# State-space rows 1-4, 6, 7: two of eight pairs get their scan inputs from GpSimd and keep their decays in PSUM

## The reference, cut to what matters

```
x, z   = split(hidden @ W_in)                    # after the norm
u      = gelu(conv4(x)), z = gelu(conv4(z))      # 4 taps along l
dt, B, C = split(u @ W_xproj)
delta  = softplus(dt @ W_dt + b_dt)
h[l]   = exp(delta[l] * A[n]) * h[l-1] + delta[l] * B[n, l] * u[l]   # per d and n
y[l]   = sum over n of C[n, l] * h[l] + D * u[l]
out    = concat(y, z) @ W_out
```

## Time and profile before

| what | value |
|---|---|
| median of 3 executions | 879.94 us (879.92 to 880.79) |
| the profiled execution, its time | 881.1 us |
| its span, first to last instruction | 879.1 us |
| mean granted TensorE clock | 0.994 |
| busy: PE, DVE, ACT, POOL | 842.9, 700.3, 556.5, 629.0 us |
| first scan starts, last scan ends | 334.7, 566.6 us |

### The profile page before, as it was taken

One profiled execution on the slowest core, in us unless ns is written; L12 is line 12 of the kernel. 1 busy time (PEld: TensorE's weight loads), 2 busy tenths in 40 slices (PEclk: granted clock), 3 DMA queues, 4 the chain that ended last, 5 costly groups with the idle time before them and its releaser, 6 DMA issues. The chain is left out here.

```text
span 879.1 us, 12640 instructions
## 1 busy us (share of the span) xinstructions
PE 842.9 (96%) x3851; PEld 638.1 (73%) x3851; DVE 700.3 (80%) x1279; ACT 556.5 (63%) x1048; POOL 629.0 (72%) x471
## 2 busy tenths in 40 slices
PE   8999999999999999889898996999999999999997
PEld 7678778877877785566565554687887888788885
DVE  6969768777976578999999999877977877786664
ACT  6665655565557669878888784365565556555554
POOL 7959676766766767768886996865767667676765
PEclk9999999999999999999999999999999999999999
DMA  8733574363434343444344444345457435436440
GB/s 213 227 114 107 154 192 120 115 154 123 135 105 124 104 129 119 158 142 157 120 171 144 134 148 145 122 132 162 112 164 198 128 116 144 159 108 183 141 121 24
DMA packets 125139, 122.40 MB, mean 139 GB/s; under 512 B 59272, under 2 KB 82960, under 8 KB 125072
## 3 DMA queue, kind: packets, MB, share of 16 engines
q1 hardware_dynamic: 102368, 116.35, 43.9%
q10 hardware_dynamic: 22704, 5.25, 2.8%
HBM read 112.40 MB, written 9.18 MB: 138 GB/s over the span
## 5 line engine op out<-in xcount | busy, mean ns | idle before, releaser
L806 POOL TENSOR_TENSOR act_lo<-act,act_hi 128x512 fp32r<-128x512 f32 x288 | 372.4, 1298 | 187.4 <-ACT act_hi L917 185.4
L910 ACT ACTIVATE bank<-bank 128x512 f32<-128x512 f32 x252 | 146.6, 582 | 234.1 <-PE bank L1245 222.8
L1141 DVE TENSOR_TENSOR sg<-bank,c_ring 128x512 f32<-128x512 f32 x252 | 172.6, 685 | 97.1 <-ACT bank L910 95.1
L1241 PE MATMUL bank<-x_parts,w_hi 128*128 128x512 f32 x572 | 231.4, 405 | 3.1 <-DVE sg L1141 2.0
L1119 DVE SCALAR_TENSOR_TENSOR act<-sg,bank 128x512 f32<-128x512 f32 x288 | 197.9, 687 | 40.9 <-PE bank L1245 20.5
L1242 PE MATMUL bank<-x_parts,w_lo 128*128 128x512 f32 x572 | 226.2, 395 | 0.0
L1245 PE MATMUL bank<-x_parts,w_hi 128*128 128x512 f32 x572 | 226.2, 395 | 0.0
L917 ACT ACTIVATE act_hi<-act 128x512 fp32r<-128x512 f32 x286 | 178.1, 623 | 0.4 <-PE bank L1217 0.4
L1241 PEld LDWEIGHTS bank<-x_parts,w_hi 128*128 128x128 f32 x572 | 107.5, 188 | 35.2 <-issue 4.8
L1245 PEld LDWEIGHTS bank<-x_parts,w_hi 128*128 128x128 f32 x572 | 107.5, 188 | 25.9
L1242 PEld LDWEIGHTS bank<-x_parts,w_lo 128*128 128x128 f32 x572 | 107.6, 188 | 25.7 <-issue 1.7
(11 more groups left out here) (181 smaller groups left out, 959.1 us busy)
## 6 DMA issues: line engine op xcount, KB each, us to landing
c_ring<-c_dram SPq DMA_DIRECT2D x252, 256.0 KB, 3.7
c_ring<-c_dram SPq DMA_DIRECT2D x64, 512.0 KB, 3.7
y_dram<-out_t SPq DMA_DIRECT2D x56, 64.0 KB, 2.8
y_tok<-y_dram SPq DMA_DIRECT2D x14, 256.0 KB, 3.7
xt_dram<-xn ACTq DMA_DIRECT2D x40, 64.0 KB, 3.4
xt<-xt_dram ACTq DMA_DIRECT2D x10, 256.0 KB, 2.9
out<-x_sb SPq DMA_DIRECT2D x7, 256.0 KB, 2.4
x_sb<-in_L_attn_hidden_states SPq DMA_DIRECT2D x3, 512.0 KB, 6.5
```

The source lines that it names most:

```text
L806: self.nc.gpsimd.tensor_tensor(m["act_lo"][:, g % LAG], m["act"][:, g % ACTS], m["act_hi"][:, g % LAG].bitcast(FP32), ALU.subtract).then_i ...
L910: nc.scalar.activation(self.h_bank[:, g % 2], self.h_bank[:, g % 2], ACT.Silu).then_inc(self.sg_ready, 1)
L1141: nc.vector.tensor_tensor(m["sg"][:, g % 2], silu, weight, ALU.mult).then_inc(self.w_done, 1)
L1241: nc.tensor.matmul(dst, m["w_hi"][:, k, n, :], x_hi, start=True, stop=False)
```

## The change

In pairs 3 and 5 of rows 1, 2, 3, 4, 6 and 7, twelve pairs in all, the roles of the two operands change places. B comes to the partitions by a DMA from DRAM into one of two new SBUF slots (`b_slots`), as C does; GpSimd multiplies the slot by du in place; ScalarE writes the decays into the PSUM bank that B's spread used; and TensorE puts a single column of zeros into that bank (a matmul of one column) in place of the two spread matmuls. VectorE does nothing for the input of such a pair. To have B in DRAM, the store of C's rows becomes a store of B's and C's rows, issued at pair 3 of the row before. GpSimd multiplies slot 0 (for pair 3) at pair 7 of the row before, slot 1 (for pair 5) at pair 1 of the same row; its du of the next row moves from pair 3 to pair 4. On ScalarE the second copy of y moves behind the decays of its step. On TensorE one tap of z's convolution moves from step 5 to step 4.

```diff
+MOVED = ((),) + ((3, 5),) * 4 + ((),) + ((3, 5),) * 2
+SLOTS = 2
...
+    def store_rows(self, sp, i):
+        sp.wait_ge(self.rows_copied, 2 * (i + 1))
+        sp.dma_start(self.c_dram[i], self.bc_rows[0:2 * NS, :]).then_inc(self.c_stored, 16)
+
+    def load_slot(self, sp, i, n):
+        if n >= len(MOVED[i]):
+            return
+        earlier = [j for j in range(i) if len(MOVED[j]) > n]
+        if earlier:
+            sp.wait_ge(self.scan_done, earlier[-1] * PAIRS + MOVED[earlier[-1]][n] + 1)
+        else:
+            sp.wait_ge(self.f1.down_done, BLOCKS)
+        pair = MOVED[i][n]
+        sp.dma_start(self.m["b_slots"][:, n].rearrange("p s l -> p (s l)"),
+                     self.c_dram[i, 2 * pair:2 * pair + 2].rearrange("s l -> (s l)").partition_broadcast(P)
+                     ).then_inc(self.slot_loaded[n], 16)
...
+                if i + 1 < BATCH:
+                    if n == 3:
+                        self.store_rows(sp, i + 1)
+                    if n == 5:
+                        sp.wait_ge(self.c_stored, 16 * (i + 2))
+                        self.load_slot(sp, i + 1, 0)
+                    if n == 7:
+                        self.load_slot(sp, i + 1, 1)
...
+    def pool_input(self, pool, i, n):
+        if n >= len(MOVED[i]):
+            return
+        uses = self.slot_uses(i, n) + 1
+        pool.wait_ge(self.slot_loaded[n], 16 * uses)
+        slot = self.m["b_slots"][:, n]
+        self.nc.gpsimd.tensor_tensor(slot, self.m["du"][:, i % 2].unsqueeze(1).broadcast_to([P, 2, SEQ]), slot, ALU.mult
+                                     ).then_inc(self.slot_ready[n], 1)
...
-                    if n == (3 if i else 4):
+                    if n == 4:
                         self.pool_du(pool, i + 1)
+                    if n == 7:
+                        pool.wait_ge(self.du_ready, i + 2)
+                        self.pool_input(pool, i + 1, 0)
+                if n == 1:
+                    self.pool_input(pool, i, 1)
...
+        if self.moved(g):
+            ae.wait_ge(self.b_ready, g + 1)
+            for s in range(2):
+                nc.scalar.activation(self.b_of(g)[:, s, s:SEQ], m["delta"][:, i % 2, s:SEQ], ACT.Exp,
+                                     scale=m["a_neg"][:, 2 * n + s:2 * n + s + 1]).then_inc(self.decay_ready, 1)
+            return
...
+                if RING <= g + 1 < ALL_PAIRS and self.moved(g + 1):
+                    self.act_decays(ae, g + 1)
+                if RING <= g + 2 < ALL_PAIRS and not self.moved(g + 2):
+                    self.act_decays(ae, g + 2)
                 if n == 4 and i - 1 in TURNED:
                     self.act_back_y(ae, i - 1)
-                if RING <= g + 2 < ALL_PAIRS:
-                    self.act_decays(ae, g + 2)
...
+                if self.moved(g):
+                    slot = self.slot_of(g)
+                    dve.wait_ge(self.slot_ready[slot], self.slot_uses(i, slot) + 1)
+                    decays, added = self.b_of(g)[:], self.m["b_slots"][:, slot]
+                else:
+                    dve.wait_ge(self.in_done, self.inputs_before(g + 1))
+                    decays, added = self.decay[:, g % RING], self.b_of(g)[:]
...
+        if self.moved(g):
+            pe.wait_ge(self.zeroed, 1)
+            self.nc.tensor.matmul(self.b_of(g)[:, 1, 0:1], m["ident"][:, :], self.decay[:, 0, 0, 0:1], start=True,
+                                  stop=True).then_inc(self.b_ready, 1)
+            return
...
+                    if n == 4 and i:
+                        self.pe_conv(pe, i, 1, [1], self.z_bank(i))
                     if n == 5 and i:
-                        self.pe_conv(pe, i, 1, [1, 2], self.z_bank(i))
+                        self.pe_conv(pe, i, 1, [2], self.z_bank(i))
```

More of the change, by code:

```diff
@@ L108, in program @@
         act_hi = sb("act_hi", [P, LAG, SEQ], F32R)
+        with nc.sbuf_tensor("b_slots", [P, SLOTS, 2, SEQ], FP32) as b_slots:
+            pass
         act_lo = sb("act_lo", [P, LAG, SEQ], F32R)
@@ L117, in program @@
         xt_dram = nc.dram_tensor("xt_dram", (2, BATCH, D, SEQ), FP32, kind="Internal").ap()
-        c2_dram = nc.dram_tensor("c2_dram", (BATCH, NS, SEQ), FP32, kind="Internal").ap()
+        c2_dram = nc.dram_tensor("c2_dram", (BATCH, 2 * NS, SEQ), FP32, kind="Internal").ap()
         th = sb("th", [P, 2, P])
@@ L1382, in __init__ @@
         self.c_loaded = [sem(f"c_loaded{n}") for n in range(RING)]
+        self.slot_loaded = [sem(f"slot_loaded{n}") for n in range(SLOTS)]
+        self.slot_ready = [sem(f"slot_ready{n}") for n in range(SLOTS)]
         self.delta_ready, self.du_ready = sem("delta_ready"), sem("du_ready")
@@ L1399, in b_of, with moved, slot_of, slot_uses @@
         return self.b_bank[g % 2] if g else self.m["bank"][2]
+    def moved(self, g):
+        return g % PAIRS in MOVED[g // PAIRS]
+    def slot_of(self, g):
+        return MOVED[g // PAIRS].index(g % PAIRS)
+    def slot_uses(self, i, n):
+        return sum(len(pairs) > n for pairs in MOVED[:i])
+    def inputs_before(self, g):
+        return sum(not self.moved(j) for j in range(g))
+    def store_rows(self, sp, i):
[13 more added lines that the diff above has]
+                     ).then_inc(self.slot_loaded[n], 16)
     def load_c(self, sp):
         m = self.m
+        self.store_rows(sp, 0)
+        sp.wait_ge(self.c_stored, 16)
         for i in range(BATCH):
-            sp.wait_ge(self.rows_copied, 2 * (i + 1))
-            sp.dma_start(self.c_dram[i], self.bc_rows[NS:2 * NS, :]).then_inc(self.c_stored, 16)
-            sp.wait_ge(self.c_stored, 16 * (i + 1))
             for n in range(PAIRS):
@@ L1415, in load_c @@
                 sp.dma_start(slot.rearrange("p s l -> p (s l)"),
-                             self.c_dram[i, 2 * n:2 * n + 2].rearrange("s l -> (s l)").partition_broadcast(P)
+                             self.c_dram[i, NS + 2 * n:NS + 2 * n + 2].rearrange("s l -> (s l)").partition_broadcast(P)
                              ).then_inc(self.c_loaded[n % RING], 16)
+                if i + 1 < BATCH:
[6 more added lines that the diff above has]
+                        self.load_slot(sp, i + 1, 1)
     def pool_low_rows(self, pool, r):
@@ L1713, in dve_pairs @@
                 dve.wait_ge(self.decay_ready, 2 * g + 2)
-                dve.wait_ge(self.in_done, g + 1)
+                if self.moved(g):
[5 more added lines that the diff above has]
+                    decays, added = self.decay[:, g % RING], self.b_of(g)[:]
                 need(dve, self.sum_done, g - RING + 1)
@@ L1717, in dve_pairs @@
                     dve.wait_ge(self.f1.down_done, BLOCKS if g else BLOCKS - 2)
-                nc.vector.tensor_tensor_scan(flat(self.state(g)), flat(self.decay[:, g % RING]),
-                                             flat(self.b_of(g)[:]), 0.0, ALU.mult, ALU.add
+                nc.vector.tensor_tensor_scan(flat(self.state(g)), flat(decays), flat(added), 0.0, ALU.mult, ALU.add
                                              ).then_inc(self.scan_done, 1)
```

## The result

The changed kernel took a median of 882.52 us (880.89 to 883.78, 12 executions), the kernel before 879.97 us (878.69 to 882.57, 12 executions): a ratio of 1.0025, 95% interval 1.0015 to 1.0035. It is slower by 0.25%. The forecast was 871.2, so 11.3 us are to be explained.

The account below looks back on a forecast made before the run. VectorE was taken to pace rows 1 to 6, and row 7 until TensorE's last wait. Gains of 10.2 us, less 2.6 for GpSimd, plus 1.15 in row 7 gave 8.75, so 871.2 us by the median, range 868.5 to 874.

Parts of the forecast that it names:

- ACT: ScalarE's queue, rows 1 to 4: same number of exponentials, moved decays ready about in time; 0.5 us charged.
- signs of being wrong: Among them: VectorE waiting for ScalarE or TensorE over 1 us in every row; moved scans or inputs over 2.4 us.
- VectorE: Each moved pair loses its 1.30 us input, 10.4 us over rows 1 to 4; a moved scan keeps 2.20.
- PE: TensorE: a one-column matmul, taken as 0.2 us, replaces two spread matmuls; step 5 fits with 0.1 us to spare.
- The clock: Rows 1 and 4: two VectorE waits for the spread may go with less TensorE idle time; one counted, 1.3 us.
- POOL: GpSimd needs 25.8 us a row; 1.0 charged in rows 3 and 4, and 2.6 at row 7's routing step.
- my sum: Gain of 10.2 us in rows 1 to 4, less 2.6 at the routing step, plus 1.15 in row 7: 8.75.
- The rows turn to PE and ACT: Rival, rows 1 to 4: overruns of 1.2 us a row leave 5.4, and 4.0 at the end: 876; chance 0.20.
- The slower rival: Moved scans and GpSimd exclude each other in SBUF, 2.2 us per moved scan: about 13 slower, 893; chance 0.05.

Follow-up runs that it names:

- the version with both orders mended: Changed kernel with free decays queued ahead of moved ones and, in row 7, the first copy of y ahead of pair 59's decays: 872.57 us, ratio 0.9916.
- the version with both taps back: Changed kernel with both taps of z's convolution in step 5 again, as before the change: 880.12 us, ratio 0.9999.
- the column by ScalarE: Changed kernel with ScalarE writing the column of zeros itself after scan g-2, without TensorE's one-column matmul: 874.68 us, ratio 0.9935.

## Why the prediction was wrong

**The step that failed** is "ACT". I wrote that "the exponentials keep their number", checked that each moved decay is ready before its scan, and charged 0.5 us. For the moved decay itself that is nearly right: VectorE waited for one only once in rows 1 to 6, 1.3 us. What I didn't price is the queue behind the wait. In order: the column of pair 5 isn't ready until scan 3 has ended and PE has worked through to its step 4; ScalarE waits 3.6 there; the decays of pair 6, the second copy of y and the norm's work follow in order, and only then the gelus and the next row's exponentials. I started the long chain at the projection of step 5, which "moves 0.9 earlier with the tap", with a shortfall of 0 to 0.3. It really started at the column: in row 2 it ran for 21.7 us (404.80 to 426.48) with 0.9 of rest, and VectorE waited 1.7 to 1.8 at its end in four rows (7.0 in all, for the 0.5 that I charged), which is one of the signs of being wrong that I had written down. With only the order of this queue changed the kernel takes 874.35.

**Row 7, the same step.** I asked of the second copy of y, which the change moves, whether it is in time, and did not ask it of the first, which the diff doesn't touch but which now stands behind a decay that waits. Mended alone it was worth 4.0 us.

**VectorE.** Right: 12 inputs gone, moved scans at 2.27 beside weightings at 2.36.

**PE.** The column was sized well enough: its two records together take 0.28 us with the granted clock at the 2.4 GHz level (1.00 at 404.42 in row 2), and 0.58 at the 1.2 GHz level (0.50 at column 59 in row 7), where I took 0.2 and at most 0.46. The point was its latency, as I wrote, but I looked for it in step 5 and in VectorE's wants, not in ScalarE's.

**The clock.** Mis-sized, in the change's favour: I counted one stall of 1.3; the tap on the kernel before removes all three, 3.6 in the profile and 2.65 between the medians. In the changed kernel the granted clock fell at other places, each behind new idle time of PE: in row 3's projection (2.10 idle, 0.59 from 419.35 to 423.50) and more than before in row 7 (0.82, for 0.95 in the earlier trace rows).

**POOL.** Mechanism right. Its busy share was 100% in row 1, 97% in row 2 (26.22 of 27.10), 98% in row 3 and 92% in row 4, where I had written over 95% from row 1 on. In the changed kernel the wait before the routing step was 1.45, not 4 to 6, since the rows came late by themselves; once ScalarE's order was mended it was 2.6 to 3.5, and the step itself 2.3, near the 2.0 of the forecast. In the version with both orders mended scan 57 stood 8.1 ahead of the kernel before, where my sum has 10.2 - 2.6 = 7.6. That moving pairs in rows 6 and 7 brings a loss of 2.8 I had not foreseen.

**Rivals.** "The rows turn to PE and ACT" described rows 1 to 4 (6.8 at pair 40, for its 5.4), but its price left ScalarE's queue in row 7 out and gave 876. The slower rival, exclusion by the SBUF ports, is void for decays in PSUM, as written; without PSUM it is real. What made the kernel slower had no rival of its own.

**Open.** The version that changes only ScalarE's order, 872.57, stands 1.4 above the forecast. That it comes so near is in part luck: at spread 62, where my sum has a gain of 8.75, its profile shows 8.1; the tap alone on the kernel before shows 3.6 there, for the 1.3 that I counted. If the two add, the moved pairs brought about 4.5 (an estimate) for the 7.45 of my sum. Why the version with both taps back is faster than the changed kernel is not shown. I didn't run the column by ScalarE with rows 1 to 4 alone.

## What to carry to other kernels

When an instruction gets a new wait, being ready for its own consumer is the smaller question: list what stands behind it in its engine's queue, up to the next thing that another engine wants, and shift all of that by the wait, at each place where the pattern occurs, irregular rows first. Put work whose operands are long ready ahead of work that waits, and let the waiting engine wait for the true source (the scan) and not for an engine that passes it on in its own order. And where four engines are within 3 us of each other in a 27 us row, as in row 2 after the change, taking work from one needs a timeline of the other three, not their busy sums.

## What the runs showed of the hardware

A scan with two SBUF operands beside GpSimd can lose more than one weighting lasts: it took up to 6.73 us, where a scan in the other form takes 2.27, so it lost 4.5, and a weighting takes 2.36; in that time three of GpSimd's instructions went by. GpSimd loses too: one weighting took 4.33. GpSimd's product of 128x1024 took 2.40 us in the mean with the slot as its second operand and 1.90 with du twice: the shape of the operands is not all that sets it. A routing step of 16 columns beside GpSimd's products took 2.0 to 2.3 us in every run. And moving less than a microsecond of matmuls to an idle place of PE (the tap) removed three stalls together, 2.65 us between the medians; two of them had come with a fall of the granted clock, to 0.51 in row 1 and to 0.66 from 466.50 to 471.00 in row 4.
